# A mixture-of-experts phase recut: 21 blocks of 128 places in place of 14 of 256, with the weights coming in half slabs

## The reference, cut to what matters

```
x = hidden_states.reshape(-1, HIDDEN)                      # 896 rows of 256
logits = SOFTCAP * jnp.tanh((x @ wg.T) / SOFTCAP)          # 8 experts
topk_vals, topk_ids = jax.lax.top_k(jax.nn.softmax(logits), 2)
topk_w = topk_vals / jnp.sum(topk_vals, axis=-1, keepdims=True)
route = zeros.at[row, topk_ids].set(topk_w)
h1 = jnp.einsum('th,eih->tei', x, w1)                      # w1, w3: 8 x 1024 x 256
h3 = jnp.einsum('th,eih->tei', x, w3)
act = jax.nn.gelu(h1, approximate=False) * h3
expert_out = jnp.einsum('tei,ehi->teh', act, w2)           # w2: 8 x 256 x 1024
out = jnp.einsum('teh,te->th', expert_out, route)
x = x + jnp.tanh(g_ffn[2]) * out
```

## Time and profile before

| | us |
|---|---|
| profiled execution, its own time | 1392.34 |
| its span | 1390.6 |
| first product of the expert blocks starts | 812.99 |
| last addition to x of the phase ends | 1114.55 |
| PE busy over the span | 1204.5 (87%) |
| DVE busy | 857.2 (62%) |
| ACT busy | 672.0 (48%) |
| POOL busy | 532.2 (38%) |

### The profile page before, as it was taken

One profiled execution on the slowest core, in us unless ns is written; L12 is line 12 of the kernel. 1 busy time (PEld: TensorE's weight loads), 2 busy tenths in 40 slices (PEclk: granted clock), 3 DMA queues, 4 the chain that ended last, 5 costly groups with the idle time before them and its releaser, 6 DMA issues. The chain is left out here.

```text
span 1390.6 us, 25468 instructions
## 1 busy us (share of the span) xinstructions
PE 1204.5 (87%) x9571; PEld 954.4 (69%) x9571; DVE 857.2 (62%) x1973; ACT 672.0 (48%) x1512; POOL 532.2 (38%) x536
## 2 busy tenths in 40 slices
PE   3999999999997697689999469889888859999876
PEld 2677777777775265556777469889887747777544
DVE  6664555555554346667787556666666476777676
ACT  3355444455452221257666234554454136666565
POOL 3355554555553000288887431110100441271132
PEclk9999999999998798889999579999999979999987
DMA  6000000000001151300110355556662260000000
GB/s 181 12 2 12 12 1 12 12 1 1 2 1 29 30 157 41 91 22 23 44 32 2 126 189 167 189 173 200 182 198 83 61 192 24 13 13 2 1 7 21
DMA packets 60090, 88.96 MB, mean 64 GB/s; under 512 B 8673, under 2 KB 49905, under 8 KB 59969
## 3 DMA queue, kind: packets, MB, share of 16 engines
q1 hardware_dynamic: 57856, 81.82, 19.3%
q0 software_dynamic: 2112, 5.51, 1.4%
HBM read 81.81 MB, written 5.51 MB: 63 GB/s over the span
## 5 line engine op out<-in xcount | busy, mean ns | idle before, releaser
L906 POOL TENSOR_SCALAR a_arena<-a_arena 112x487 f32<-112x487 f32 x128 | 192.7, 1516 | 176.9 <-DVE a_arena L1117 176.9
L1198 ACT ACTIVATE a_arena<-banks,a_arena 112x487 f32<-112x487 f32 x128 | 84.2, 663 | 193.0 <-DVE a_arena L1111 193.0
L1111 DVE TENSOR_REDUCE a_arena<-banks 112x2 f32<-112x974 f32 x64 | 75.0, 1172 | 102.6 <-PE banks L997 102.6
L93 PE MATMUL banks<-f_x_high,f_up_high 128*128 128x256 f32 x448 | 128.4, 287 | 3.6 <-DVE f_up_low L2010 2.2
L94 PE MATMUL banks<-f_x_low,f_up_high 128*128 128x256 f32 x448 | 128.0, 286 | 0.0
L95 PE MATMUL banks<-f_x_high,f_up_low 128*128 128x256 f32 x448 | 128.0, 286 | 0.0
L397 POOL TENSOR_TENSOR a_arena<-a_arena 112x375 f32<-112x375 f32 x128 | 114.7, 921 | 24.1 <-ACT a_arena L704 23.9
L513 PE MATMUL banks<-ident,a_arena 112*126 112x112 f32 x768 | 105.5, 274 | 12.0 <-POOL a_arena L397 9.6
L513 PEld LDWEIGHTS banks<-ident,a_arena 112*126 112x126 f32 x768 | 77.2, 143 | 46.0 <-issue 27.6
L2052 POOL DMA_INDIRECT f_arena<-f_rows,f_arena x28 | 32.7, 1167 | 190.8 <-PE banks L2090 172.7
L2216 DVE TENSOR_TENSOR f_arena<-banks,f_arena 128x512 f32<-128x512 f32 x56 | 38.6, 689 | 107.4 <-ACT f_arena L2192 107.4
(11 more groups left out here) (341 smaller groups left out, 3314.0 us busy)
## 6 DMA issues: line engine op xcount, KB each, us to landing
f_arena<-in_L_ffn_w1T SPq DMA_DIRECT2D x14, 1024.0 KB, 5.8
f_arena<-in_L_ffn_w3T SPq DMA_DIRECT2D x14, 1024.0 KB, 4.9
f_arena<-in_L_ffn_w2T SPq DMA_DIRECT2D x14, 1024.0 KB, 5.9
a_arena<-in_ctxT SPq DMA_DIRECT2D x24, 375.0 KB, 5.0
a_arena<-in_ctx SPq DMA_DIRECT2D x16, 375.0 KB
f_y<-f_arena SPq DMA_DIRECT2D x14, 256.0 KB, 5.1
a_arena<-in_L_xattn_Wkv SPq DMA_DIRECT2D x2, 1024.0 KB, 9.9
a_arena<-in_fside_BxSxS SPq DMA_DIRECT2D x8, 164.1 KB, 2.4
```

Of the source, the lines that this page charges most:

```text
L93: pe.matmul(out, sh, mh, start=start, stop=False)
L906: pool.tensor_scalar(z, z, inv[:, n % 4, s:s + 1], None, ALU.mult).then_inc(p_ready, 1)
L1111: dve.tensor_reduce(negmax[:, n % 4, :], banks[0:T, 0:2, 0:KEYS], AX, ALU.max, negate=True).then_inc(max_ready, 1)
L1198: act.activation(prob[n % PR][s][:, 0:KEYS], banks[0:T, s, 0:KEYS], ACT.Exp, bias=negmax[:, n % 4, s:s + 1], accum_out=total[:, n % 4, s:s ...
```

## The change

The blocks are cut to SIZE = 128 places, and BLOCKS = (1792 + 8 x 128 - 1) / 128 = 21. Each block still needs all three slabs of its expert. What changes for a block:

- A slab is loaded in two halves (`PART`), w1 and w3 by hidden numbers 0 to 511 and 512 to 1023, so that six transfers of 512 KB make a block (three of 1 MB before). Rows of w1 and w3 are now 2 KB long in a transfer (4 KB before), those of w2 1 KB as before. The halves go round a ring of RING = 10 buffers.
- In `up(k, j)` the operands are swapped: the 128 places are stationary and 512 hidden numbers of the weights are moving. It is 24 products of 512 columns a block. The result has places along the partitions, so the gated hidden numbers must be turned back: `turn_hidden` is new, 4 transposes for each half.
- `down(k)` is 24 products of 256 columns.
- Low parts of w2 are now made by POOL, in two pieces of 512 for each half, for every block; those of w1 and w3 by DVE.
- A block's rows come by one gather, and POOL issues it for block k+1 ahead of its work on block k's w2.
- The last LATE = 2 blocks are returned by PE with `spread`. The weight of each place is now in `spread`, for which `Assignment` makes a list of weights by place (three bf16 parts, 16 small products).

The core of the diff:

```
-    SIZE = 256
-    HALVES = SIZE // P
+    SIZE = P
+    LATE = 2
+    HI = I // 2
+    QC = HI // P
+    PART = SLAB // 2
+    RING = 10
...
+        def low_weights(eng, k, i, parts=1):
+            high, rest = rounded_parts(k, i)
+            whole = raw_part(k, i)
+            eng.wait_ge(w_high, 6 * k + i + 1)
...
+            op.then_inc(w_low_pool if k == 0 or i > 3 else w_low_dve, 1)
...
+                for i, z in enumerate(("L2_ffn_w1T", "L2_ffn_w3T") * 2 + ("L2_ffn_w2T",) * 2):
+                    n = 6 * k + i
+                    if n >= RING:
+                        wait_low(sp, (n - RING) // 6, (n - RING) % 6)
...
-            for k in range(2, BLOCKS):
-                gather(k)
+            for k in range(BLOCKS):
+                if 0 < k < BLOCKS - 1:
+                    gather(k + 1)
+                low_weights(pool, k, 4, 2)
+                low_weights(pool, k, 5, 2)
...
+            def up(k, j):
+                n = 2 * k + j
...
+                for s, ps in enumerate((ps1, ps3)):
+                    wait_low(pe, k, 2 * j + s)
+                    for c in range(DC):
+                        mm = split_product(pe, ps[n % 2], [z[:, c, :] for z in xs[k % 2]],
+                                           [w[:, s, c, j * HI:(j + 1) * HI] for w in up_w[k % 2]],
+                                           start=(c == 0), stop=(c == DC - 1))
...
+            def turn_hidden(n):
+                pe.wait_ge(gated_done, n + 1)
+                if n > 1:
+                    pe.wait_ge(h_low, n - 1)
+                for c in range(QC):
+                    mm = pe.transpose(psH[n % 2][:, c * P:(c + 1) * P], gated[n % 2][:, c * P:(c + 1) * P], ident[:])
...
             for k in range(BLOCKS):
...
+                up(k, 0)
+                if k:
+                    turn_hidden(2 * k - 1)
+                if k + 1 < BLOCKS:
+                    turn(k + 1)
+                up(k, 1)
+                if k:
+                    down(k - 1)
+                turn_hidden(2 * k)
...
             for k in range(BLOCKS):
...
+                split(k, 4)
+                gelu(2 * k)
+                split(k, 5)
+                if k:
+                    high_hidden(2 * k - 1)
+                if more:
+                    high_rows(k + 1)
+                    split(k + 1, 0)
+                    split(k + 1, 1)
+                gelu(2 * k + 1)
+                if more:
+                    split(k + 1, 2)
+                    split(k + 1, 3)
...
+                high_hidden(2 * k)
...
+                gate(2 * k)
+                if k:
+                    low_hidden(2 * k - 1)
...
+                if more:
+                    low_rows(k + 1)
+                    low_weights(dve, k + 1, 0)
+                    low_weights(dve, k + 1, 1)
+                gate(2 * k + 1)
+                if more:
+                    low_weights(dve, k + 1, 2)
+                    if k:
+                        move(k - 1)
+                    low_weights(dve, k + 1, 3)
+                low_hidden(2 * k)
```

More of the change, by code:

```diff
@@ L1759, in __init__ @@
         self.row_b = m.sb("r_row_b", [T, size], BF16)
-        self.last_w, self.last_weight = m.sb("r_last_w", [T, 2, B]), m.sb("r_last_weight", [T, B])
+        self.part = [m.sb(f"r_part{j}", [T, 2 * B], BF16) for j in range(3)]
+        self.remain = [m.sb(f"r_remain{j}", [T, 2 * B]) for j in range(2)]
+        self.weights, self.slot_weight = m.sb("r_weights", [T, 2 * B, 3, late], BF16), m.sb("r_slot_weight", [P, late])
         self.slot_index = m.sb("r_slot_index", [T, 2 * B], I32)
@@ L1835, in tensor_lists, with tensor_weights @@
         mm.then_inc(self.s_listed, 1)
+    def tensor_weights(self, pe):
+        pe.wait_ge(self.s_parts_made, 3)
+        for n in range(2 * B):
+            mm = pe.matmul(self.psW, self.hot[:, n, 0:P], self.weights[:, n].rearrange("t j h -> t (j h)"),
+                           start=(n == 0), stop=(n == 2 * B - 1))
+        mm.then_inc(self.s_weights_listed, 1)
     def scalar(self, act):
@@ L1896, in vector @@
         total = self.psC[:, B * E:(B + 1) * E]
[L1897 to L1898 removed]
+        stepped(dve.tensor_tensor(self.over, total.unsqueeze(2).to_broadcast([T, E, self.spans - 1]),
+                                  self.starts[:, 1:self.spans].unsqueeze(1).to_broadcast([T, E, self.spans - 1]), ALU.is_gt))
         settle()
@@ L1943, in vector @@
         dve.tensor_scalar(self.token, self.token_f, -1.0, 0.0, ALU.add, ALU.max).then_inc(self.s_token_made, 1)
+        whole = self.best.rearrange("t k b -> t (k b)")
+        dve.wait_ge(self.s_weighted, 1)
+        for j in range(3):
+            stepped(dve.tensor_copy(self.part[j], whole))
+            settle()
+            if j < 2:
+                stepped(dve.tensor_tensor(self.remain[j], whole, self.part[j], ALU.subtract))
+                whole = self.remain[j]
+                settle()
+            dve.tensor_tensor(self.weights[:, :, j, :], self.inside[:, :, K - self.late:K],
+                              self.part[j].unsqueeze(2).to_broadcast([T, 2 * B, self.late]), ALU.mult
+                              ).then_inc(self.s_parts_made, 1)
+        dve.wait_ge(self.s_weights_listed, 1)
+        dve.tensor_reduce(self.slot_weight, self.psW.rearrange("p (j h) -> p h j", j=3), AX, ALU.add
+                          ).then_inc(self.s_slot_weighted, 1)
 def sparse_ffn(nc, st, xT, io):
@@ new lines, in raw_part, with wait_low @@
+        def raw_part(k, i):
+            whole = raw[(6 * k + i) % RING]
+            return whole.rearrange("p (c i) -> p c i", c=QC if i > 3 else DC)
+        def wait_low(eng, k, i):
+            if k and i < 4:
+                eng.wait_ge(w_low_dve, 4 * (k - 1) + i + 1)
+            else:
+                eng.wait_ge(w_low_pool, 2 * k + i + 1)
+        def low_weights(eng, k, i, parts=1):
+            high, rest = rounded_parts(k, i)
+            whole = raw_part(k, i)
+            eng.wait_ge(w_high, 6 * k + i + 1)
+            c = whole.shape[1] // parts
```

311 lines of the change are left out of this document (137 added, 174 removed).

## The result

The changed kernel took 1343.86 us (median of four runs, 1342.36 to 1346.29) against 1393.93 (median of four) for the kernel before. The ratio is 0.966, with a 95% interval of 0.960 to 0.971. The profiled execution took 1346.29 us. Predicted were 1348 us, range 1324 to 1372.

The account below looks back on a forecast made before the run. Mutually excluding subtractions of POOL and DVE, 10.8 us plus 0.6 idle, were to set a period of 11.4 us. The phase would end 44.6 us earlier: 1392.34 - 44.6 = 1347.7 us, range 1324 to 1372.

Parts of the forecast that it names:

- the start: Before the first product of the expert phase: one gather waited for instead of two, first product 3.3 us earlier, at 809.7.
- the gathers and additions: End of the phase: 16 final gathers pace DVE's additions, 25.2 us from first gather to last addition, as before.
- changes between kinds of work: PE in each block: an estimated 0.1 us for each of four changes, within a sum of 9.9 us.
- The DMA term: Transfers of a block: weights, gathered and stored rows take 9.2 us, with 390 GB/s taken for 2 KB rows.
- The wait for psY: PE before the down products: its 2.0 us of idle time a block, behind moves out of bank psY, go.
- What holds the block up: POOL's and DVE's subtractions exclude each other: 10.8 us a block that can't overlap, plus 0.6 idle, period 11.4 us.
- the second coupling: Row gather on POOL behind four subtractions: a chain over two blocks asking 10.6 us a block, 11.7 with slow gathers.
- rival 2: PE's stalls feed on themselves, or DMA is slower than thought: period 12 to 13.6 us, 1360 to 1392 us; 17%.
- the signs that the prediction named for being right: Gelu period 11 to 12 us, some stretched subtractions, no psY wait, PE waiting for row gather or weights' low parts.
- rival 3: Transfers don't keep up, DMA share near 1, ACT waiting for weights: slower than before, 1408 us at 237 GB/s; 6%.
- Rival 4: Transfers don't overlap, each half paying its own start: 3.7 us a half, 22 us for six, slower by some 165; 2%.
- The prediction's price for that rule: Batching transfers to 1 MiB or more: six halves one at a time take 19 us a block, slower by some 150.

Follow-up runs that it names:

- e2: Changed kernel with POOL's subtractions for w2's low part cut to one column from block 2 on; 1325.9 us, ratio 0.943 to the kernel before.
- e8: Early gathers (e1) with a ring of 6 half slabs in place of 10; 1332.6 us, ratio 0.949 to the kernel before.
- e9: Early gathers (e1) with one low part of w3 a block moved from DVE to POOL; 1353.8 us, ratio 0.962 to the kernel before.
- e1: Changed kernel with four buffers of rows in place of two, each gather issued two blocks earlier; 1328.5 us, ratio 0.946 to the kernel before.
- e4: Changed kernel with w2's low part made by DVE instead of POOL, which keeps the gathers; 1322.6 us, ratio 0.942 to the kernel before.
- e11: e6 with w2 brought by one transfer of 1 MB instead of two of 512 KB; 1320.6 us, ratio 0.939 to the kernel before.
- e5: Changed kernel as it is, run again beside the experiments on the same chip as e6; 1349.1 us, ratio 0.962 to the kernel before.
- e6: Early gathers (e1) with w2's low part shared, first half by DVE, second by POOL; 1318.5 us, ratio 0.940 to the kernel before.
- e3: Changed kernel with each half slab's transfer bringing half its bytes from block 2 on; 1330.4 us, ratio 0.948 to the kernel before.

## Why the prediction was right, and which step of it was not

**The total.** 1347.7 was worked out and the profiled execution took 1346.29. The last addition was predicted at 1070.0 and ended at 1070.01, but by terms that made up for each other: the stages ahead of the phase +4.7 us; the start -1.4; first product to last block's gelu 228.1 against 230.8, -2.7; to the first final gather 5.1 against 4.3, +0.8; the gathers and additions 23.9 against 25.2, -1.3. Without the first of these the addition would have ended 4.7 us before the time predicted. What follows the phase took 276.3 us, where it had been 277.8.

**Engine by engine.** The product of 512 columns took 0.23 us as taken. PE's whole block is 9.5 us (e2), not 9.9: the 0.4 for changes between kinds of work don't exist. ACT's copy took 1.06 against 1.04, DVE's gate 0.68 against 0.69. The DMA term of 9.2 us can't be read from this kernel: 308 GB/s at a share of 0.91 would be 338 at full share and 10.1 us for 3.41 MB, but e2 brought the same bytes in every 9.5 us, and the changed kernel itself moved 396 GB/s from 930 to 934 us. So the share is no linear measure here, and the term was at most 0.3 us too small. It stayed hidden by the ring of ten (e8).

**The wait for psY** went entirely, and of the two things that the prediction named as PE's next wait, row gather and low parts, it was the first.

**What holds the block up: here a step failed.** "Per block the excluding work is POOL's 5.9 us and DVE's 4 x 1.22 = 4.9 us: 10.8 us that can't overlap." The exclusion exists (e9: a sum of 10.8 gave 11.5). But the sum of this kernel is 4 x 1.23 + 4 x 1.14 = 9.5: a subtraction occupies the engine for its distance to the next, 1.14, not for its duration, and the gather's 0.95 need hardly be counted (e1 runs at 9.7 with it; DVE's subtractions run on beside it, as the last section shows). So the exclusion alone would give about 9.7, and not 11.4. What filled the gap is the second coupling, which the prediction sized at 10.6 to 11.7 and said "lies beside the first, not on top". Its parts, on POOL's timeline in the block after the gelu at 916.06:

```profile
914.92 7.14 POOL L2050 TENSOR_TENSOR f_down_low<-f_arena,f_down_high 128x512 fp32r<-128x512 f32 x4 [2.27 <-ACT f_down_high L2216]
922.21 1.77 POOL L2094 DMA_INDIRECT f_arena<-f_rows,f_arena  x1
925.01 5.97 POOL L2050 TENSOR_TENSOR f_down_low<-f_arena,f_down_high 128x512 fp32r<-128x512 f32 x4 [1.03 <-ACT f_down_high L2216]
931.13 0.96 POOL L2094 DMA_INDIRECT f_arena<-f_rows,f_arena  x1
```

The issue comes 6.15 us after the gelu (6.0 predicted). The rows are there at 929.36, 7.15 later (5.8). The gelu behind them starts at 940.25, 10.9 later (9.3), and the clock explains that: the stretches from 929 to 934 us lack (1 - 0.61) x 4 + 0.14 = 1.7 us of full speed. 24.2 us for two blocks are 12.1 a block in the worst pair; then the gather is ahead again (0.96 on POOL at 931.13, with no subtraction of DVE under way when it began) and two faster blocks follow. Between the first and the 21st gelu PE stood 22.8 us for rows and 1.3 us for low parts, and at a mean clock of 0.95 over these 223 us some 11 us were lost to the clock: 35 / 20 = 1.8 us a block. Without stalls the 20 intervals would be one of 8.0 and 19 of 9.5, a mean of 9.4. The sum is 11.2, as measured.

So rival 2's mechanism, stalls that the clock makes longer, was at work within the size of the forecast. That a steady 11.4 from one mechanism came near a mean of 11.16 from another is luck, and the signs that the prediction named for being right (a period of 11 to 12, stretched subtractions, PE waiting for the row gather) all came without telling the two apart. The exclusion has its part in it, for it holds up both the pieces ahead of the gather and the gather. Which share of the 25 us is due to it alone these runs don't separate: e4 and e2 take both away at once.

**Rivals 3 and 4.** The DMA share of 0.91 was a sign named for rival 3; the second sign, ACT waiting for weights, didn't come. Rival 4 was not seen: halves land 5.3 to 6.4 us after issue, but several are under way at once, and 308 GB/s is far above the 142 that a lone half in 3.7 us would give. The rule of 1 MiB (the Trainium skill, DMA: Bandwidth & Descriptors, section Bandwidth, Measured) doesn't decide here, as e11 shows. The prediction's price for that rule has a slip: 19 us in place of 11.4, at 20 us of time for each, is some 150 us over the forecast, but only some 110 over the kernel before.

**Start.** The first product came 33.97 us after the phase's first transfer, where it was 812.99 - 774.35 = 38.64: -4.7 against -3.3. Its parts: first gather -1.5, and from there to the product 4.8 us in place of 8.0, since only one gather of rows is waited for.

## What to carry to other kernels

A small transfer that a slow engine issues behind its own arithmetic is a chain through that engine, whatever else bounds the loop: give it more buffers and issue it blocks ahead, which took here 2 KB per partition of a place that was already there, and added about half to what the whole change saved. When periods come out at the right mean, look at them one by one; an alternation of 9.5 and 14 us is another mechanism than a steady 11.4. A second engine's help is to be priced by what it excludes and by what queues behind it: here doing everything on DVE beat sharing as long as the gather stood behind POOL's share (e4 against e5), and no longer when it was issued early (e6).

## What the runs showed of the hardware that was not expected

- POOL's and DVE's subtractions exclude each other by whole instructions, and not in fair turns. In e9 POOL ran four pieces of 1.27 us without a break (924.30 to 929.38), while a subtraction of DVE, started at 926.23, had to stand: it alone took 4.23 us, with its next 6.46. The Trainium skill (SBUF — State Buffer, section SBUF: two separate sides) describes the port pair of the two engines as a lock that whichever starts first holds for its whole instruction. The traces agree on the whole instruction (1.97 = a wait and 1.2 in e1). When POOL's piece under way ended in e9, the turn did not pass to DVE, which was already waiting; in e1 it did, within POOL's four pieces (7.26 us in place of 5.1). What decides it is not shown.
- An indirect transfer's issue on POOL is held up too, where a subtraction of DVE is under way as it begins: 1.76 us in place of 0.95 in most blocks of e1. It doesn't hold DVE in turn: beside the issue at 931.13 in the changed kernel DVE's two subtractions, started at 931.18, took 2.36 us together, their length alone.
- TensorE's granted clock after a stall. In the changed kernel from 825 us on, the six stalls of 2.17 us and more (up to 3.38) were each followed by 3 to 4 us at 1.2 GHz with PE fully busy, and those up to 1.91 by none. In e5 it was the same for four stalls of 2.61 to 3.65 us and for those up to 1.94. A stall of 2.69 us in e3 was not followed by one, so the length of the stall does not settle it.
- Half slabs of 512 KB with the row transfers between them moved at 347 to 358 GB/s over 160 us with the DMA engines full (e1, e2, e6), and at 353 with w2 in transfers of 1 MB (e11). The changed kernel moved 396 GB/s for 4 us (930 to 934).
